# Conv attention block on one core: chains of small vector operations moved to PSUM scratch, and pieces of weights loaded a unit or more earlier

## What is computed

```
z   = layer_norm over channels (x)                       # per position
g   = group_norm(z, 32 groups) * gamma + beta            # per batch and group of 8 channels
qkv = conv1d(g, qkv_w, 16 taps, 256 -> 768 channels) + qkv_b
h   = attention(q, k, v), 4 heads of 64, 1024 positions
y   = z + conv1d(h, proj_w, 5 taps) + proj_b
x1  = x + y
out = x1 + ffn(layer_norm over channels (x1))            # ffn: x itself plus a table-like shift in a few channels
```

## Time and profile before

| | us |
|---|---|
| median of 3 runs | 1068.02 (1067.68 to 1069.91) |
| the profiled execution's own time | 1067.8 |
| its span, first to last instruction | 1066.0 |
| PE busy | 935.6 |
| DVE busy | 745.2 |
| ACT busy | 666.5 |
| POOL busy | 340.1 |

### The profile page before, as it was taken

The page is one execution under the profiler, slowest core; times in us unless marked ns, Lnnn a source line. Parts: engine busy times, 40 slices in busy tenths (PEclk is TensorE's granted clock), DMA queues, the critical chain, the costliest instruction groups (busy, mean ns, idle before and its releaser), DMA issues.

```text
span 1066.0 us, 19610 instructions
## 1 busy us (share of the span) xinstructions
PE 935.6 (88%) x7826; PEld 744.5 (70%) x7826; DVE 745.2 (70%) x1230; ACT 666.5 (63%) x1112; POOL 340.1 (32%) x225
## 2 busy tenths in 40 slices
PE   2586679988999779999998999999999989999864
PEld 1475567756877557777776778877788768777653
DVE  6999876654674467878777565566557566778877
ACT  5756366566566547867787666576657666576631
POOL 2766642331352025526550121110112105323320
PEclk9989799989999989999999999999999999999987
DMA  7040133756677754747544754735465862452412
GB/s 282 29 181 22 60 114 98 182 135 182 155 198 167 180 157 104 155 116 211 144 105 79 181 128 94 154 93 110 98 162 109 228 164 59 111 129 68 112 60 80
DMA packets 291866, 138.32 MB, mean 130 GB/s; under 512 B 269120, under 2 KB 271552, under 8 KB 291264
## 3 DMA queue, kind: packets, MB, share of 16 engines
q1 hardware_dynamic: 291776, 137.08, 51.0%
HBM read 48.80 MB, written 16.95 MB: 62 GB/s over the span
## 4 chain that ended last, share of the span: by engine, by line
PE 36%; DVE 32%; ACT 15%; issue 8%; DMA 5%; SPq 2%; POOL 1%; ACTq 0%; DVEq 0%; POOLq 0%
PE cM L1233 9%; PE cQ L1233 8%; PE cP L1233 8%; DVE W L1513 5%; ACT arena L1109 5%; DVE smx L1708 4%; DMA wsum<-w_qkv 4%; DVE arena L1685 4%; PE psS L1370 3%; PE psT L1370 3%; PE psV L1347 2%; SPq L535 2%; ACT arena L914 2%; PE psV L1351 2%; DVE arena L1559 1%
## 5 line engine op out<-in xcount | busy, mean ns | idle before, releaser
L1233 PE MATMUL cM<-U,W 128*128 128x256 f16 x1728 | 207.6, 278 | 30.7 <-DVE U L1521 18.1
L1233 PEld LDWEIGHTS cM<-U,W 128*128 128x128 f16 x1728 | 171.1, 99 | 65.6 <-DVE U L1521 18.4
L1233 PE MATMUL cQ<-U,W 128*128 128x256 f16 x1728 | 207.8, 277 | 8.9 <-DVE W L1513 6.2
L1233 PE MATMUL cP<-U,W 128*128 128x256 f16 x1728 | 204.2, 276 | 8.7 <-DVE W L1513 4.9
L1233 PEld LDWEIGHTS cQ<-U,W 128*128 128x128 f16 x1728 | 170.2, 99 | 42.9 <-DVE W L1513 6.8
L1233 PEld LDWEIGHTS cP<-U,W 128*128 128x128 f16 x1728 | 169.5, 98 | 41.4 <-ACT y_all L969 4.9
L1685 DVE SCALAR_TENSOR_TENSOR arena<-arena,smx 128x1024 f16<-128x1024 f32 x128 | 174.8, 1366 | 14.8 <-ACT arena L1119 14.4
L724 POOL TENSOR_TENSOR ap<-ap 128x512 f32<-128x512 f32 x24 | 39.7, 1655 | 397.7 <-ACT ap L981 397.5
L1119 ACT ACTIVATE arena<-arena,smx 128x1024 f16<-128x1024 f32 x128 | 147.0, 1148 | 4.3
L1708 DVE TENSOR_REDUCE smx<-psS 128x1 f32<-128x1024 f32 x64 | 78.0, 1218 | 60.1 <-PE psS L1370 59.7
L1102 ACT ACTIVATE smx<-smx,tiny 128x1 f32<-128x1 f32 x128 | 37.3, 291 | 125.3 <-DVE smx L1708 124.9
(11 more groups left out here) (215 smaller groups left out, 1329.9 us busy)
## 6 DMA issues: line engine op xcount, KB each, us to landing
U<-kept_u SPq DMA_DIRECT2D x21, 520.0 KB, 5.7
staging<-w_qkv SPq DMA_DIRECT2D x20, 512.0 KB, 5.7
wsum<-w_qkv SPq DMA_DIRECT2D x24, 256.0 KB, 4.1
U<-kept_u SPq DMA_DIRECT2D x7, 780.0 KB, 5.0
kept_u<-temp_b SPq DMA_DIRECT2D x9, 520.0 KB, 3.5
arena<-x_tok SPq DMA_DIRECT2D x8, 512.0 KB, 6.8
arena<-arena SPq DMA_DIRECT2D x16, 256.0 KB, 3.6
W<-x_tok SPq DMA_DIRECT2D x4, 1024.0 KB, 5.7
```

The lines of the kernel that those rows point to most:

```text
L1233: last = mm(out, W[:, j, wl, c, QTAPS * (3 * family + third) + tap, :], u[:, ul, c, at + tap:at + tap + QUART], start=((g, c, t) in OPENER ...
```

## The change

Three things.

1. The scratch of the chains of step 0 lies in PSUM: `early`, `early_a` and `early_b` are columns 384 to 419 of psV. Instructions of a chain that had two inputs in SBUF have one in SBUF and one in PSUM, or both in PSUM. The layer norm's result is copied to `ln` by an added instruction, on which nothing in the chain waits.
2. Where two inputs in SBUF were left, TENSOR_TENSOR became TENSOR_SCALAR with one column as a scalar: L1438 and L1439, each over 2 columns and in a row, become two instructions of one column that don't wait for each other; so do L1446 and L1447. L1465 and L1478 (one column) too.
3. Pieces of weights are loaded in units 1 to 12 of the attention beside step 1 (before: 3 to 14), and in units 0 to 11 of that beside step 2 (before: 3 to 14). They are squared in slots 3 to 14 of step 1 and 2 to 13 of step 2 (before: 4 to 15). So a piece that was squared one slot behind the unit of its load is squared two slots behind it.

```diff
+        early = psV[:, 3 * P:3 * P + 30].rearrange("p (r k) -> p r k", r=3)
+        early_a, early_b = (psV[:, 3 * P + 32 + CT * q:3 * P + 32 + CT * (q + 1)] for q in range(2))
...
-        def rstd_ask(var, eps, at, asked):
-            nc.vector.tensor_scalar(nt[:, 0, at:at + var.shape[-1]], var, eps, None, ALU.add).then_inc(S[asked], 1)
-        def rstd_end(ch, eng, out, at, sq_done, runs):
+        def rstd_ask(var, eps, work, asked, sign=1.0):
+            nc.vector.tensor_scalar(work[:, 0, :], var, sign, eps, ALU.mult, ALU.add).then_inc(S[asked], 1)
+        def rstd_end(ch, eng, out, work, q, sq_done, runs):
...
-            n, s, q = (nt[:, r, at:at + out.shape[-1]] for r in range(3))
+            n, s = (work[:, r, :] for r in range(2))
...
-        SQUARES = [(n, i) for n in (1, 2) for i in range(4, 16)]
+        SQUARES = [(1, i) for i in range(3, 15)] + [(2, i) for i in range(2, 14)]
...
-                    if k in (0, 1) and 3 <= u < 15:
-                        load_chunk(12 * k + u - 3)
+                    if k in (0, 1) and 0 <= u - 1 + k < 12:
+                        load_chunk(12 * k + u - 1 + k)
...
-                rstd_end(ch, dve, ln[:, b, :, 1], 0, "ln_sq", q + 1)
+                rstd_end(ch, dve, early[:, 2, 0:8], early[:, :, 0:8], nt[:, 2, 0:8], "ln_sq", q + 1)
                 ch.end()
-                v.scalar_tensor_tensor(nmr[:, b, :], ln[:, b, :, 0], -1.0, ln[:, b, :, 1], ALU.mult, ALU.mult) \
+                v.tensor_copy(ln[:, b, :, 1], early[:, 2, 0:8]).then_inc(S["z_nm"], 1)
+                v.scalar_tensor_tensor(nmr[:, b, :], ln[:, b, :, 0], -1.0, early[:, 2, 0:8], ALU.mult, ALU.mult) \
...
-                ch.step(v.tensor_tensor(gs[:, :, 2], gs[:, :, 0], gs[:, :, 0], ALU.mult))
-                v.tensor_tensor(gs[:, :, 1], gs[:, :, 1], gs[:, :, 2], ALU.add).then_inc(S["gstat_done"], 1)
+                for c in range(CT):
+                    v.tensor_scalar(gs[:, c, 1:2], gs[:, c, 0:1], gs[:, c, 0:1], gs[:, c, 1:2], ALU.mult, ALU.add) \
+                        .then_inc(S["gstat_done"], 1)
...
-                ch.step(v.tensor_tensor(gn[:, :, 2], gn[:, :, 0], gn[:, :, 0], ALU.mult))
-                ch.step(v.tensor_tensor(gn[:, :, 3], gn[:, :, 1], gn[:, :, 2], ALU.subtract))
-                rstd_ask(gn[:, :, 3], 1e-5, 8, "gn_var")
+                for c in range(CT):
+                    ch.done(v.tensor_scalar(gn[:, c, 3:4], gn[:, c, 0:1], gn[:, c, 0:1], gn[:, c, 1:2], ALU.mult, ALU.subtract))
+                ch.wait()
+                rstd_ask(gn[:, :, 3], 1e-5, early[:, :, 8:10], "gn_var", -1.0)
...
-                ch.step(v.tensor_tensor(gn[:, :, 1], gn[:, :, 1], par[:, 0, :], ALU.mult))
-                ch.step(v.tensor_tensor(gn[:, :, 2], gn[:, :, 0], gn[:, :, 1], ALU.mult))
-                ch.step(v.tensor_tensor(gn[:, :, 2], par[:, 1, :], gn[:, :, 2], ALU.subtract))
+                ch.step(v.tensor_tensor(early_a, early[:, 2, 8:10], par[:, 0, :], ALU.mult))
+                ch.step(v.tensor_tensor(early_b, gn[:, :, 0], early_a, ALU.mult))
+                ch.step(v.tensor_tensor(early_b, par[:, 1, :], early_b, ALU.subtract))
...
-                    v.tensor_tensor(am[:, 0:1], am[:, 4:5], am[:, 5:6], ALU.add).then_inc(S["wam_done"], 1)
+                    v.tensor_scalar(am[:, 0:1], am[:, 4:5], am[:, 5:6], None, ALU.add).then_inc(S["wam_done"], 1)
```

More of the change, by code:

```diff
@@ L834, in _, with sqrt @@
             a = nc.scalar.activation
-            def sqrt(asked, done, runs, width, at=0):
+            def sqrt(asked, done, runs, work):
                 act.wait_ge(S[asked], runs)
-                a(nt[:, 1, at:at + width], nt[:, 0, at:at + width], ACT.Sqrt).then_inc(S[done], 1)
+                a(work[:, 1, :], work[:, 0, :], ACT.Sqrt).then_inc(S[done], 1)
             def ln_root(q):
-                sqrt("ln_var", "ln_sq", q + 1, 8)
+                sqrt("ln_var", "ln_sq", q + 1, early[:, :, 0:8])
             def gn_root(q):
-                sqrt("gn_var", "gn_sq", q + 1, CT, 8)
+                sqrt("gn_var", "gn_sq", q + 1, early[:, :, 8:10])
             def normal(q):
                 b = BATCH_AT[q]
-                act.wait_ge(S["z_nm"], q + 1)
+                act.wait_ge(S["z_nm"], 2 * (q + 1))
                 for i in range(8):
@@ L931, in last_stage @@
                 if kind == "norm":
-                    sqrt("f_var", "f_sq", b + 1, RUNS[b][2])
+                    sqrt("f_var", "f_sq", b + 1, nt[:, :, 0:RUNS[b][2]])
                 if kind == "ob":
@@ L1161, in group_mean @@
             def group_mean(b):
-                pe.wait_ge(S["gstat_done"], b + 1)
+                pe.wait_ge(S["gstat_done"], CT * (b + 1))
                 if b:
@@ L1415, in layer_norm @@
                 ch.wait()
-                rstd_ask(ln[:, b, :, 1], 1e-6, 0, "ln_var")
+                rstd_ask(ln[:, b, :, 1], 1e-6, early[:, :, 0:8], "ln_var")
             def layer_norm_end(q):
                 ch, b = norm_chains[q], BATCH_AT[q]
-                rstd_end(ch, dve, ln[:, b, :, 1], 0, "ln_sq", q + 1)
+                rstd_end(ch, dve, early[:, 2, 0:8], early[:, :, 0:8], nt[:, 2, 0:8], "ln_sq", q + 1)
                 ch.end()
-                v.scalar_tensor_tensor(nmr[:, b, :], ln[:, b, :, 0], -1.0, ln[:, b, :, 1], ALU.mult, ALU.mult) \
+                v.tensor_copy(ln[:, b, :, 1], early[:, 2, 0:8]).then_inc(S["z_nm"], 1)
+                v.scalar_tensor_tensor(nmr[:, b, :], ln[:, b, :, 0], -1.0, early[:, 2, 0:8], ALU.mult, ALU.mult) \
                     .then_inc(S["z_nm"], 1)
-            group_chains = [Chain(dve, "c_g", b, 19) for b in range(NB)]
+            group_chains = [Chain(dve, "c_g", b, 18) for b in range(NB)]
             def group_stats(b):
@@ L1445, in group_norm @@
                                       psV[:, 0:2 * CT].rearrange("p (k c) -> p k c", k=2)))
[L1446 to L1448 removed]
+                for c in range(CT):
+                    ch.done(v.tensor_scalar(gn[:, c, 3:4], gn[:, c, 0:1], gn[:, c, 0:1], gn[:, c, 1:2], ALU.mult, ALU.subtract))
+                ch.wait()
+                rstd_ask(gn[:, :, 3], 1e-5, early[:, :, 8:10], "gn_var", -1.0)
             def group_norm_end(b):
                 ch = group_chains[b]
[L1452 to L1455 removed]
+                rstd_end(ch, dve, early[:, 2, 8:10], early[:, :, 8:10], nt[:, 2, 8:10], "gn_sq", b + 1)
+                ch.step(v.tensor_tensor(early_a, early[:, 2, 8:10], par[:, 0, :], ALU.mult))
+                ch.step(v.tensor_tensor(early_b, gn[:, :, 0], early_a, ALU.mult))
+                ch.step(v.tensor_tensor(early_b, par[:, 1, :], early_b, ALU.subtract))
                 wait(dve, "eo_done", 4 * b)
[L1457 to L1458 removed]
+                ch.done(v.tensor_scalar(ab[:, :, 0], early_a, usc[:, 0:1], None, ALU.mult))
+                v.tensor_scalar(ab[:, :, 1], early_b, usc[:, 0:1], None, ALU.mult).then_inc(S["ab_done"], 1)
                 ch.end()
@@ L1477, in w_scale @@
                 pow2(ch, top[:, m:m + 1], WK, wsc[:, 0, m:m + 1], wsc[:, 1, m:m + 1], squared=True)
-                v.tensor_tensor(isc[:, m:m + 1], wsc[:, 1, m:m + 1], usc[:, 1:2], ALU.mult) \
+                v.tensor_scalar(isc[:, m:m + 1], wsc[:, 1, m:m + 1], usc[:, 1:2], None, ALU.mult) \
                     .then_inc(S["wsc_done"], 1)
@@ L1617, in last_stage @@
                 if kind == "norm":
-                    rstd_ask(stats[:, :, 1], 1e-5, 0, "f_var")
-                    rstd_end(ch, dve, stats[:, :, 1], 0, "f_sq", run + 1)
+                    rstd_ask(stats[:, :, 1], 1e-5, nt[:, :, 0:count], "f_var")
+                    rstd_end(ch, dve, stats[:, :, 1], nt[:, :, 0:count], nt[:, 2, 0:count], "f_sq", run + 1)
                     ch.step(v.scalar_tensor_tensor(nmr[:, b, i0:i0 + count], stats[:, :, 0], -1.0, stats[:, :, 1], ALU.mult,
```

## The result

The changed kernel takes **1025.55 us** (median of 4 runs, 1025.43 to 1026.02) against 1067.85 for the kernel before on the same chip: a ratio of 0.9601, 95% interval 0.9584 to 0.9617. That is 42.3 us less, where 38.9 were forecast. The profiled execution took 1025.49, 1.8 over its span of 1023.7.

A forecast was written before the change was run, and what follows sets the result against it. PE was taken as the bound, except DVE in step 0 and, in steps 1 and 2, ACT's waits for late pieces. 1067.8 - 28.9 (pieces) - 10 (chains) = 1028.9, forecast 1029 us, range 1019 to 1048.

The forecast's parts named there:

- the likeliest case: Whole kernel: both parts gain as costed, within their bounds, 1020 to about 1040 us; chance 0.60.
- The pieces: Steps 1 and 2: loading weights a slot further ahead ends ACT's waits; gain 28.9 us, bounds 14.5 to 33.
- Step 1: Step 1 takes 102.1 us: 98.0 as in step 6, 2.5 waiting for activations, 1.6 lost clock at its start.
- Step 2: Step 2 takes 101.5 us: 98.0, plus 1.5 scales' spread, 1.5 second tile's bank, 0.5 small waits.
- Rival A: Steps 1 and 2: pieces still land late, half the excess stays, 14.4 us gained instead of 28.9: 1043; chance 0.15.
- The chains: Step 0: small DVE operations with PSUM scratch no longer wait for POOL; gain 10 us, bounds 3 to 15.
- My sum by clusters: Step 0: gains from rows of DVE waits for POOL, 3.9, 2.3, 4.5 and 3.0 for smaller ones, 13.7 us in all.
- the first cluster: Step 0, 86.04 to 90.92: four DVE waits for POOL in a row, followed by single-input statistics; all 3.9 us gained.
- the third cluster: Step 0, 110.16 to 118.37: six DVE waits, 6.3 us over, a weight operation in their midst; 4.5 us gained.
- PSUM at no price: Step 0 chains: a PSUM source costs DVE no more than SBUF, 0.15 us; the skill's fixed cost would add 4.4 us.
- B: Step 0: the wait for POOL moves to DVE's next weight operation, gain 3 us instead of 10: 1036; chance 0.14.
- C: Steps 1 and 2: SP's loads wait for ACT's squares, 44 us on the queue, 15 us worse: 1073; chance 0.03.

The follow-up runs named there:

- distance or place: The changed kernel with its loads of pieces one unit later and the squares where they are: 1051.57 us, 0.9866 of the kernel before.
- the columns alone: The kernel before with only the one-column scalar forms of the chain operations, all scratch left in SBUF: 1065.56 us, 0.9998 of the kernel before.
- the chains alone: The changed kernel with loads and squares of the pieces put back where they were before: 1049.82 us, 0.9848 of the kernel before.
- the probe: No attention: DVE runs twelve each of eight small operation forms, POOL silent, then beside POOL additions; two SBUF inputs took 0.63 us each against 0.20.

## Why the prediction was right, and where its steps were off

The result is inside the likeliest case: both parts work by the mechanism that was named, and the time is 3.5 us under the forecast. Some terms were off by as much or more, and partly cancelled.

**The pieces.** 28.9 forecast, 28.6 measured for steps 1 and 2 (17.6 + 11.0). The mechanism is shown: the slot more is what counts (distance or place), and "so I expect PE" was right, with 96.66 of 98.8 and 99.90 of 105.0. The two steps were each mis-sized, and both came out beside the 100 to 104 that were to be seen: step 1 gave 3.3 us more than forecast, step 2 3.5 less. That their sum is within 0.3 is luck.

- *Step 1*, forecast 102.1, took 98.8. "98.0" came from step 6, which has eight groups of second products on PE within its bounds where step 1 has seven; that is about 1.4 us less. The earlier trace rows had it, with 835 against 850 products, so "the same matrix work" was wrong for step 1. These lines of PE, in step 1 after and in step 6 before (busy us, mean ns), say so:

```profile
L1349 PE MATMUL psV<-arena 128*128 128x256 f16 x56 | 7.3, 273 | 0.0
```
```profile
L1347 PE MATMUL psV<-arena 128*128 128x256 f16 x64 | 8.3, 273 | 0.0
```

  The 2.5 for activations stayed, as 2.1. The 1.6 of lost clock at the start did not: it is 1.00 there now. I had put that loss down to step 0's idle time. It came back just as well behind the old step 0 with only the loads changed, and was lost behind the new one when the loads were a unit later. The first convolution products of step 1 on PE, in turn for the kernel before, the changed kernel, only the loads, and loads a unit later:

```profile
159.10 5.77 PE L1233 MATMUL cM<-U,W 128*128 128x256 f16 x36 [2.46 <-issue]
```
```profile
143.41 4.11 PE L1235 MATMUL cM<-U,W 128*128 128x256 f16 x36 [2.14 <-issue]
```
```profile
158.38 4.11 PE L1233 MATMUL cM<-U,W 128*128 128x256 f16 x36 [2.19 <-issue]
```
```profile
143.68 5.76 PE L1235 MATMUL cM<-U,W 128*128 128x256 f16 x36 [2.58 <-issue]
```

  The same 36 products take 4.11 or 5.77 us. Of the twelve traces with these products, four have them long: the kernel before, the same with the columns alone and with `load_eo` moved, and the changed kernel with the loads a unit later. The wait ahead of them does not sort them (2.19 is long with the columns alone, 2.51 is short with the chains alone). The kind of step 0 does not either, though it may tilt the odds: long in three of four with the old one, in one of eight with the new. What tips it stays open; it is worth 1.6 us.

- *Step 2*, forecast 101.5, took 105.0. The 1.5, 1.5 and 0.5 of small waits vanished with ACT's lag: with `load_eo` moved, the step takes 98.4 with PE busy throughout. In their place stood the wait of 5.1 behind `load_eo` and, with a clock of 0.98 in the step, 1.5 us more of PE for the same 853 instructions (99.90 against 98.38): together the 6.6 between the two. The prediction asked "what is late next" of the engines alone. Rival A had the right ingredient, a transfer among transposing transfers that takes longer, but for the pieces. Those land as fast as before:

```profile
wsum<-w_qkv SPq DMA_DIRECT2D x24, 256.0 KB, 4.1
```

**The chains.** 10 forecast, 15.4 measured in step 0 (15.6 with the chains alone). This is the term that was mis-sized. My sum by clusters was 13.7, from which I took off 3.7 for waits that would move to the weight operations. DVE's lead over the kernel before can be read from the starts of equal operations. In the kernel before, then in the changed one: a reciprocal ahead of the first cluster, the statistics behind it, and the weight operation behind the third cluster.

```profile
85.85 0.15 DVE L259 RECIPROCAL nt<-nt 128x2 f32<-128x2 f32 x1
...
91.62 2.70 DVE L1408 BATCH_NORM_STATS2 st<-arena 128x6 f32<-128x256 f32 x8
...
119.46 0.75 DVE L1513 SCALAR_TENSOR_TENSOR W<-wsum,tiny,W 128x512 f16<-128x512 f32 x1
```
```profile
84.09 0.17 DVE L261 RECIPROCAL nt<-psV 128x2 f32<-128x2 f32 x1
...
85.96 2.70 DVE L1410 BATCH_NORM_STATS2 st<-arena 128x6 f32<-128x256 f32 x8
...
103.94 1.00 DVE L1518 SCALAR_TENSOR_TENSOR W<-wsum,tiny,W 128x512 f16<-128x512 f32 x1
```

The lead is 1.8 us at the reciprocal (small ones, of 3.0 forecast for the whole step), 5.7 at the statistics: 3.9 for the first cluster, to the tenth as forecast. At the weight operation behind the second (102.99 in the earlier trace rows, 92.39 now) it is 10.6, and 9.9 when that operation is over, since it took 1.97 instead of 1.28: 4.2 instead of 2.3. I had let the weight operation wait until 100.7, as if POOL's schedule stood still while DVE's moved; it met another operation of POOL's for 0.7 us instead. The third cluster has its lead at 15.5: 6.0 from the copy that opens it (109.98 in the earlier trace rows, 100.49 now), where 4.5 was forecast, for the same reason. And the lead of 15.5 reaches PE whole, as step 1's start, 15.4.

What I took off did happen, elsewhere: DVE's 42 weight operations rose from 52.4 us to 55.6, the 128x512 pieces out of the arena for one:

```profile
L1518 DVE SCALAR_TENSOR_TENSOR W<-arena,tiny,W 128x512 f16<-128x512 f32 x4 | 5.7, 1476 | 0.0
```

They had been 3.8 us, 999 ns each. With three other two-input operations (1.8 us more) that is 5.0 us moved on. But DVE's busy time in step 0 still fell from 134.2 to 120.1, 14.1 us, so what the small operations gave up was 19 us, more than my clusters held. The clock has no visible part in this: over step 0 it was granted 0.91 in the kernel before and 0.96 in the changed one, but 0.88 when the changed kernel was run again, and that step 0 took 139.0 us. The forecast of step 1's start, 142 to 148, missed 139.4.

**PSUM at no price.** Right: 0.17 us from PSUM in the kernel, and 2.44 against 2.35 for twelve in the probe. The Trainium skill, "VectorE: DVE Perf Modes", section on the TRN2 errata, has 120 cycles fixed for PSUM to SBUF and 58 for SBUF to SBUF, 62 cycles or an estimate of 65 ns more, from which the prediction had 4.4 us in all. Its table has no case for a result in PSUM, which 44 of the 68 operations have. Like with like is the reciprocal over 8 columns, with its result in SBUF: 190 ns from SBUF before, 197 from PSUM now. So here the measurement decides against the page.

**Rivals.** A fell: ACT's wait is 6.0, under the 8 named. B's mechanism is real, seen pure in the columns alone, and smaller than the gain; of its two signs neither came, with fewer weight operations of 2 us and over and step 1 at 139.4. The Trainium skill, "SBUF — State Buffer", section on who interferes with whom, describes it as a lock on a port pair that DVE shares with GpSimd; the probe agrees that two SBUF inputs are held, with 6.91 for eleven such operations against 2.35 for twelve. C's waits are 1.8 us in four times as the change stands, need the squares a slot later to grow, and are then free, where the prediction had them at 44 us on PE's path. Steps 3 to 7 stayed as they were to within 1.1 us each.

## What to carry to other kernels

A load that is issued only when some other unit is through has less time than the table of slots suggests. Count from its issue in the trace to its user; here one slot gave 1.3 us against 4.1 to land, two gave all of it back, and one fewer than that lost all of it again. A wait for a shared resource is not removed by changing the operation that shows it: it moves to the next one that needs the resource. So take a chain out whole: one piece of it gave nothing (0.9998), that piece on top of the rest 4 us. And when a lag goes, look for what it covered: here a 1 MB load ahead of a small urgent transfer, free before (1.0004) and worth 5 us after.

## What was not expected of the hardware

- A scalar operation with a pointer scalar over 2 or 8 columns in SBUF took 1.2 us each beside POOL against 0.26 alone (14.82 and 3.15 for twelve), twice as bad as two tensor inputs. One column with two pointer scalars was not held at all (3.67 both times), nor was the reciprocal over 8 or 2 columns (2.67).
- A transposing transfer 1.2 us behind a load of 1040 KB took 9.45 us to land; 4.75 us behind it, in the kernel before, 4.92. With the load behind the transfer, SP was through its issue in 2.96 us instead of 7.15.
- The same 36 products at the start of step 1 run at one clock level or partly at the other with hardly a difference in what PE did before, and what decides it was not found.

Not tried: taking the weight operations, which now carry the contention, out of POOL's way.
